# Two fused linear layers on one core: another order of ScalarE's and VectorE's work in batches 1 and 2

## The chip, the cores and the metric

The kernel runs on one core of one Trainium2 chip. A core has a matrix engine (TensorE, PE in the profile), three elementwise engines (VectorE or DVE, ScalarE or ACT, GpSimd or POOL) and a queue (SyncE, SP) that here only issues DMAs. Each engine takes its own list of instructions in the order in which the program wrote it, and waits on counters (semaphores) that the others raise. The metric is the device time of one launch in microseconds (us). Before the change it is 382.21 us, the median of 3 runs (381.04 to 382.56).

## The reference

For each of 8 batches, x is 256 x 1024 in float32. Two residual layers follow each other:

```python
sign = 2 * mask - 1                       # int32 mask, 1024 x 1024 for each batch
x = x + (x @ W0.T + b0 + (x @ sign) * coeff[batch])
A, B = lora_As[id[batch]], lora_Bs[id[batch]]      # 1024 x 16 and 16 x 1024
x = x + (x @ W1.T + b1 + (x @ A) @ B * 2.0)
```

## The kernel before

**Arithmetic.** A float32 operand is split into a high part (rounded to the type float32r, which the matrix engine takes) and a low part (the rest), and a product is the sum high*high + high*low + low*high. ScalarE makes nearly all high parts, VectorE the low parts; every low part waits for its high part. The residual is folded in as the identity added to the weights ("diagonal" blocks, added by GpSimd at line 389, or by VectorE in `w22_diagonal`).

**Layer 0** of a batch needs its own weights, because the mask is the batch's own: W0 + 2*coeff*mask - coeff. They come in 8 units of 128 x 1024, through a ring of 6 slots. For each unit, VectorE makes the sum (`weights_sum`, line 999), ScalarE the high part (`weights_high`, line 702), VectorE the low part (`weights_low`, line 1009), and the matrix engine uses it (lines 519 and 525). Units 0 to 3 give the first half of the output y, units 4 to 7 the second. A slot's next transfer is issued when the matrix engine has read the slot. The ready y leaves the matrix engine's banks by `y_copy` (ScalarE, L740) and `y_sum` (VectorE, L1081), and is split by `y_high...` (ScalarE, L748 in batch 1, L758 later) and `y_low...` (VectorE, L1087 in batch 1, L1116 later). The second halves of the batch's banks wait for the copies of the batch before (`z_copy`, L780).

**Layer 1** multiplies y by W1. In batches 0 and 1 it does that plainly, from batch 2 on by Strassen's scheme in Winograd's form, with 7 block products in place of 8 (L550); they use T1 to T4, which are sums and differences of quarters of W1. These are made once, in batches 1 and 2, each in two halves c = 0, 1: `t_sum` (VectorE, L1057), `t_high` (ScalarE, L724), `t_low` (VectorE, L1062). In the Winograd layer of batch 2, the products take T3 second, T4 fourth, T1 fifth and T2 sixth. `t_lo_done` counts the low parts, so the list `T_ORDER` has to name the order in which they are made.

**The low-rank part.** The matrix engine makes h = y @ A (L561), between the products. ScalarE scales and splits h by three small instructions (`h_high`, L765), VectorE makes its low part (`h_low`, L1122), and then one product for each output block adds h @ B and closes the block (`close`, L591). GpSimd prepares A and B's low parts (`lora_a_diff` L401, `lora_a_low` L406, `lora_b_low` L415), between two ScalarE instructions, `lora_a_high` (L792) and `lora_b_copy` (L800). `z_copy` (batches 0 and 1) moves a closed block out of its bank.

The order on each engine is written out by hand for batches 0 to 2, and by `next_high` and `next_low` with the loops behind them for the rest. The change touches only the hand-written lists for batches 1 and 2; the lists of PE, GpSimd and SP stay as they are.

Of the kernel before, what the change touches and what calls it, by code (L numbers as in the profile page):

```python
# [17 lines left out]
def cond_residual_two_layers(nc, x, cols, slot_ids, mask, w0, w1, b1, lora_a, lora_b, out):  # L18
# [11 lines left out]
    KT = XG * PAIR  # L30
# [17 lines left out]
    W11, W12, W21, W22, T1, T2, T4 = range(7)  # L48
    T3 = W12
    T_SUMS = [(T1, k) for k in range(HT)] + [(T3, 0), (T2, 0), (T3, 1), (T2, 1), (T4, 0), (T4, 1)]  # L50
    T_ORDER = [(T1, 0), (T1, 1)] + [(t, c) for c in range(2) for t in (T2, T3, T4)]

    with ExitStack() as ctx:
        def sb(name, shape, dt):
# [642 lines left out]
        def _(act):  # L697
            def weights_high(b, k):
                e = entry(b, k)
                for lo, hi in ((0, HALF), (HALF, D)) if b == 0 and k < HALVED else ((0, D),):  # L700
                    act.wait_ge(sum_done, parts(b, k, lo // HALF))
                    act.activation(wc_hi[:, e % RING, lo:hi], sums[:, e % RING, lo:hi], ACT.Identity,  # L702
                                   bias=coeff_neg[:, b:b + 1]).then_inc(wc_hi_done, 1)
# [12 lines left out]
            def t_high(t, c):  # L716
                act.wait_ge(t_sum_done, t_sums(t, PAIR * c + 1 if t == T1 else c))
                if t == T3:
                    act.wait_ge(w12_read, 1)
                elif t == T4:  # L720

                    act.wait_ge(t_lo_done, t_count(T3, c))
                ks = slice(PAIR * c, PAIR * (c + 1))
                act.activation(w1_two[0][:, t, ks, :], t_raw(t)[:, ks, :], ACT.Copy).then_inc(t_hi_done, 1)  # L724

            def x_high(b, g):
                g = pair(b, g)
                act.wait_ge(x_in[g], 16 * (b + 1))
                act.activation(x_two[:, g, 0], x_raw[:, g], ACT.Copy).then_inc(x_hi_done, 1)  # L729
# [30 lines left out]
            def h_high(b):  # L760

                act.wait_ge(h_full, b + 1)
                hs = h_bank(b)[:].rearrange("p (s n t) -> p n s t", s=ST, n=2)
                for lo, hi, n in ((0, 2 * R, 0), (2 * R, 4 * R, 1), (B_HI, B_ALL, 0)):
                    act.activation(by_rows(h_stack[lo:hi, :]), hs[0:hi - lo, n], ACT.Copy,  # L765
                                   scale=SCALING).then_inc(h_hi_done, 1)
# [9 lines left out]
            def z_copy(b, i):  # L776
                act.wait_ge(z_full, 4 * b + z_place(b, i))
                s, _ = z_rows_of(b, i)
                need(act, z_out[s], 16 * b)
                act.activation(z_piece(b, i), layer1_bank(b, i)[:], ACT.Copy).then_inc(z_done, 1)  # L780
# [70 lines left out]
            x_high(1, 0)  # L851
            x_high(1, 1)
            weights_high(1, 1)
            x_high(1, 2)
            x_high(1, 3)
            h_high(0)
            weights_high(1, 2)
            weights_high(1, 3)
            for i in range(4):
# [22 lines left out]
            y_high_pair(1, 2)  # L882
            y_high_pair(1, 3)
            lora_b_copy(1, 1)
            t_high(T2, 0)
            for u in range(3):
                weights_high(2, u)
            h_high(1)
            weights_high(2, 3)
            for g in range(XG):  # L890
                x_high(2, g)
            t_high(T3, 0)
            z_copy(1, 0)
            weights_high(2, 4)
            z_copy(1, 1)
            t_high(T4, 0)
            weights_high(2, 5)
            z_copy(1, 2)
            t_high(T2, 1)
            t_high(T3, 1)  # L900
            z_copy(1, 3)


            weights_high(2, KT - 2)
# [6 lines left out]
            y_copy(2, 3)  # L911
            y_high(2, Y11)
            y_high(2, S3)
            t_high(T4, 1)
            lora_a_high(2)


# [66 lines left out]
        def _(dve):  # L984
# [207 lines left out]
            w1_low(HT + 3)  # L1192
            x_low(1, 0)
            weights_low(1, 0)
            x_low(1, 1)
            h_low(0)
            weights_low(1, 1)
            weights_sum(1, 2)
            x_low(1, 2)
# [18 lines left out]
            t_sum(T3, 0)  # L1218
            t_sum(T2, 0)
            t_low(T1, 0)  # L1220


            for o in range(HT, KT):
                y_sum(1, o)
            w22_diagonal(1)
            t_sum(T3, 1)
            y_low_pair(1, 2)
            y_low_pair(1, 3)
            weights_sum(2, 0)
            t_sum(T2, 1)  # L1230
            weights_sum(2, 1)
            weights_low(2, 0)
            weights_sum(2, 2)
            weights_low(2, 1)
            weights_low(2, 2)
            h_low(1)
            weights_sum(2, 3)
            t_sum(T4, 0)
            for g in range(XG):
                x_low(2, g)  # L1240
            weights_low(2, 3)
            t_low(T1, 1)
            t_sum(T4, 1)
            t_low(T2, 0)
            weights_sum(2, 4)
            t_low(T3, 0)
            weights_low(2, 4)
            weights_sum(2, 5)
            t_low(T4, 0)
            weights_low(2, 5)  # L1250


            weights_sum(2, KT - 2)
            t_low(T2, 1)
            weights_low(2, KT - 2)
            weights_sum(2, KT - 1)
            for o in range(HT):
                y_sum(2, o)
            y_add(2, S3)
            weights_low(2, KT - 1)  # L1260
            t_low(T3, 1)
            y_low(2, Y11)
            y_low(2, S3)


            for o in range(HT, KT):
                y_sum(2, o)
            y_add(2, S1)
            t_low(T4, 1)
            y_low(2, V12)  # L1270
            y_add(2, S2)
            y_low(2, Y22)
            y_low(2, S1)
# [84 lines left out]
```

## Time and profile before

| | before |
| --- | --- |
| median of 3 runs | 382.21 us |
| the profiled execution, its own time | 381.96 us |
| its span, first to last instruction | 379.0 us |
| granted TensorE clock | 1.000 of full speed |
| PE busy | 370.2 us (98%) |
| DVE busy | 310.0 us (82%) |
| ACT busy | 204.6 us (54%) |
| POOL busy | 93.2 us (25%) |
| DMA | mean 250 GB/s |

Times in the timeline are us from the span's start. A row of the timeline has the start, the time from the first start to the last end, the engine, the source line, the operation with its tiles and shapes, and the count. A bracket at its end gives the idle time of the engine before it, and what ended that. A matrix product's own duration holds about 0.16 us of pipeline that the next product overlaps, so what a wait costs is read from start to start. Batch 1's first layer starts at 59.5 us, its second at 81.9; batch 2's first layer at 107.7, its second at 131.2.

### The profile page before, as it was taken

The page shows a single profiled execution, that of the slowest core. Times are in us where ns is not written, and L with a number is a line of the kernel's source. Part 1 is how long each engine was busy: PE and PEld are TensorE (multiplying, and loading weights), DVE is VectorE, ACT ScalarE, POOL GpSimd, SP SyncE. Part 2 cuts the span into 40 slices and gives each one's busy share as a digit, 9 for nine tenths or more (in the row PEclk, how much of TensorE's full clock was granted, in tenths as well). Part 3 has the DMA queues.
Part 4 walks back from the last instruction along what each step waited for, and adds up shares of the span by engine and source line. Part 5 has one row for each costly group of instructions (what it writes and reads, how often), then busy time and mean ns, then how long its engine had stood idle before and what let it go on. Part 6 is the DMA issues. An engine that isn't in the chain of part 4 may idle for free.

```text
span 379.0 us, 5435 instructions
## 1 busy us (share of the span) xinstructions
PE 370.2 (98%) x1934; PEld 311.7 (82%) x1934; DVE 310.0 (82%) x372; ACT 204.6 (54%) x315; POOL 93.2 (25%) x116
## 2 busy tenths in 40 slices
PE   7999999999999999999999999999999999999996
PEld 7889977887787887888788887888878887888875
DVE  4998899988999899976897769965999659987613
ACT  5583865656547577347652666524673366526520
POOL 1355660434004521033100350012300431002300
PEclk9999999999999999999999999999999999999999
DMA  8999999999539587495937959297884969473002
GB/s 249 389 386 341 384 386 331 309 370 315 211 106 305 203 293 261 138 346 198 339 145 247 350 177 359 81 285 270 266 297 124 329 216 335 164 253 129 0 0 111
DMA packets 47691, 94.73 MB, mean 250 GB/s; under 512 B 3610, under 2 KB 4658, under 8 KB 47666
## 3 DMA queue, kind: packets, MB, share of 16 engines
q1 hardware_dynamic: 44848, 85.73, 67.1%
q10 hardware_dynamic: 2754, 8.66, 5.7%
q8 instruction: 15, 0.25, 0.3%
q14 instruction: 10, 0.08, 0.1%
q0 software_dynamic: 64, 0.01, 0.0%
HBM read 86.00 MB, written 8.39 MB: 249 GB/s over the span
## 4 chain that ended last, share of the span: by engine, by line
PE 79%; DVE 7%; DMA 5%; issue 4%; ACT 2%; SPq 1%; POOL 1%; DVEq 0%; ACTq 0%; POOLq 0%
PE bank L550 30%; PE bank L519 22%; PE bank L525 11%; PE bank L599 6%; PE bank L561 3%; DMA ring_raw<-in_w 3%; DVE ring_raw L999 3%; PE bank L467 2%; PE bank L591 2%; DMA ring_raw<-in_mask 1%; PE bank L474 1%; ACT ring L702 1%; DVE ring L1009 1%; POOL ring_raw L389 1%; DVE x_two L1068 1%
## 5 line engine op out<-in xcount | busy, mean ns | idle before, releaser
L550 PE MATMUL bank<-w_two,y_two 128*128 128x512 f32 x600 | 141.5, 390 | 0.1
L702 ACT ACTIVATE ring<-ring_raw,coeff_neg 128x1024 fp32r<-128x1024 f32 (+1 forms) x68 | 75.0, 1103 | 115.1 <-DVE ring_raw L999 114.6
L550 PEld LDWEIGHTS bank<-w_two,y_two 128*128 128x128 f32 x600 | 111.6, 188 | 23.9 <-issue 0.3
L519 PE MATMUL bank<-x_two,ring 128*128 128x512 f32 x448 | 127.1, 394 | 0.8 <-ACT z_rows L780 0.8
L389 POOL TENSOR_TENSOR ring_raw<-ring_raw,ident 128x128 f32<-128x128 f32 x64 | 46.8, 752 | 222.2 <-DMA ring_raw<-in_w 221.9
L999 DVE SCALAR_TENSOR_TENSOR ring_raw<-ring_raw,coeff_two 128x1024 f32<-128x1024 int32 (+1 forms) x68 | 84.9, 1261 | 15.0 <-DMA ring_raw<-in_mask 12.8
L1009 DVE SCALAR_TENSOR_TENSOR ring<-ring_raw,coeff_neg,ring 128x1024 fp32r<-128x1024 f32 (+1 forms) x68 | 84.1, 1245 | 9.7 <-ACT ring L702 9.0
L519 PEld LDWEIGHTS bank<-x_two,ring 128*128 128x128 f32 x448 | 78.0, 189 | 12.8 <-ACT z_rows L780 1.2
L525 PE MATMUL bank<-x_two,ring 128*128 128x256 f32 x448 | 78.0, 281 | 0.0
L525 PEld LDWEIGHTS bank<-x_two,ring 128*128 128x128 f32 x448 | 70.6, 189 | 8.3
L1081 DVE TENSOR_TENSOR y_raw<-bank,y_raw 128x256 f32<-128x256 f32 x56 | 20.7, 418 | 21.1 <-ACT y_raw L740 21.1
L1116 DVE TENSOR_TENSOR y_two<-y_raw,y_two 128x512 fp32r<-128x512 f32 x42 | 31.3, 767 | 5.3 <-ACT y_two L758 5.2
L415 POOL TENSOR_TENSOR b_stack<-b_raw,b_tmp 16x512 fp32r<-16x512 f32 x16 | 25.5, 1593 | 21.1 <-ACT b_tmp L800 20.5
L758 ACT ACTIVATE y_two<-y_raw 128x512 fp32r<-128x512 f32 x42 | 24.8, 625 | 4.6 <-DVE y_raw L1081 3.4
L740 ACT ACTIVATE y_raw<-bank,cols_all 128x256 f32<-128x256 f32 x56 | 21.9, 470 | 2.9 <-PE bank L525 2.8
L599 PE MATMUL bank<-w_two,y_two 128*128 128x512 f32 x96 | 22.6, 391 | 0.0
L1068 DVE TENSOR_TENSOR x_two<-x_both,x_two 128x512 fp32r<-128x512 f32 x32 | 21.7, 702 | 0.6 <-ACT x_two L729 0.6
L599 PEld LDWEIGHTS bank<-w_two,y_two 128*128 128x128 f32 x96 | 17.8, 188 | 4.0 <-DVE w_two L1025 0.4
L467 PE MATMUL bank<-x_two,ring 128*128 128x256 f32 x128 | 18.5, 285 | 1.2 <-ACT ring L702 0.7
L729 ACT ACTIVATE x_two<-x_both 128x512 fp32r<-128x512 f32 x32 | 18.3, 615 | 2.1 <-DMA x_both<-in_x 2.1
L774 ACT ACTIVATE z_rows<-bank 128x512 f32<-128x512 f32 x18 | 10.7, 597 | 15.5 <-PE bank L550 15.3
L1143 DVE TENSOR_TENSOR z_rows<-bank,z_rows 128x512 f32<-128x512 f32 x24 | 15.9, 684 | 3.7 <-PE bank L591 3.7
(50 smaller groups left out, 241.6 us busy)
## 6 DMA issues: line engine op xcount, KB each, us to landing
ring_raw<-in_w SPq DMA_DIRECT2D x60, 512.0 KB, 8.6
ring_raw<-in_mask SPq DMA_DIRECT2D x60, 512.0 KB, 9.7
x_both<-in_x SPq DMA_DIRECT2D x31, 256.0 KB, 4.0
out<-z_rows ACTq DMA_DIRECT2D x15, 512.0 KB, 7.5
w_raw<-in_w SPq DMA_DIRECT2D x12, 512.0 KB, 11.4
b_raw<-in_lora_b SPq DMA_DIRECT2D x8, 448.0 KB, 3.6
ring_raw<-in_w SPq DMA_DIRECT2D x8, 256.0 KB, 6.1
ring_raw<-in_mask SPq DMA_DIRECT2D x8, 256.0 KB, 6.2
```

The costliest lines, as they stand in the source:

```text
L389: ins = pool.tensor_tensor(blk, blk, ident[:], ALU.add)
L415: pool.tensor_tensor(b_stack[B_HI:B_ALL, cols], b_raw[B_HI:B_ALL, cols], b_tmp[B_HI:B_ALL, :].bitcast(F32), ALU.subtract).then_inc(b_lo_do ...
L467: pe.matmul(first_bank(o), w, x_two[:, pair(0, u), n, i, :], start=(u % HT == 0 and i == 0 and n == 0), stop=False, skip_group_check=True)
L519: pe.matmul(layer0_bank(b, o)[:, 0:2 * T], w, x_two[:, k // PAIR, :, k % PAIR, :], start=(k == 0), stop=False, skip_group_check=True)
L525: ins = pe.matmul(layer0_bank(b, o)[:, 0:T], w, x_two[:, k // PAIR, 0, k % PAIR, :], start=False, stop=(k == KT - 1), skip_group_check=True)
L550: ins = pe.matmul(bank[:], y_two[:, q, k, yp, :], w1_two[wp][:, j, k, :], start=(start and k == 0 and n == 0), stop=False, skip_group_chec ...
L599: pe.matmul(layer1_bank(0, i)[:], y_two[:, PAIR * h + s, k % HT, yp, :], w1_two[wp][:, PAIR * h + half, k % HT, :], start=(k == 0 and yp = ...
L702: act.activation(wc_hi[:, e % RING, lo:hi], sums[:, e % RING, lo:hi], ACT.Identity, bias=coeff_neg[:, b:b + 1]).then_inc(wc_hi_done, 1)
L999: dve.scalar_tensor_tensor(out=sums[:, e % RING, lo:hi], in0=mask_at[:, e % RING, lo:hi], scalar=coeff_two[:, b:b + 1], in1=w0_at[:, e % R ...
L1009: dve.scalar_tensor_tensor(out=wc_lo[:, e % RING, lo:hi], in0=sums[:, e % RING, lo:hi], scalar=coeff_neg[:, b:b + 1], in1=wc_hi[:, e % RIN ...
L1068: dve.tensor_tensor(x_two[:, g, 1], x_raw[:, g], x_two[:, g, 0].bitcast(F32), ALU.subtract).then_inc(x_lo_done, 1)
L1116: dve.tensor_tensor(y_two[:, n, :, 1, :], y_raw[:, at, :, 1, :], y_two[:, n, :, 0, :].bitcast(F32), ALU.subtract).then_inc(y_lo_done, 1)
```

## The change

All moves are within ScalarE's and VectorE's lists. Batch 1: `h_high(0)` stands right behind `weights_high(1, 1)`, ahead of two parts of x, and `h_low(0)` ahead of `x_low(1, 1)`. Batch 2's preparation: `h_high(1)` comes after two of the weights' high parts instead of three, `h_low(1)` after two low parts instead of three; the four `z_copy(1, ...)` stand behind each other before `weights_high(2, 4)`; `w22_diagonal(1)` and `t_sum(T3, 1)` stand before the `y_sum`s of batch 1's second half instead of after them; `weights_sum(2, 0)` stands before `y_low_pair(1, 2)`. T2's high and low parts, which stood second, are made last, in batch 2; T3's second half comes early.

```diff
@@ -48,7 +48,7 @@
     W11, W12, W21, W22, T1, T2, T4 = range(7)
     T3 = W12
     T_SUMS = [(T1, k) for k in range(HT)] + [(T3, 0), (T2, 0), (T3, 1), (T2, 1), (T4, 0), (T4, 1)]
-    T_ORDER = [(T1, 0), (T1, 1)] + [(t, c) for c in range(2) for t in (T2, T3, T4)]
+    T_ORDER = [(t, c) for t in (T1, T3, T4, T2) for c in range(2)]
 
     with ExitStack() as ctx:
         def sb(name, shape, dt):
@@ -851,9 +851,9 @@
             x_high(1, 0)
             x_high(1, 1)
             weights_high(1, 1)
+            h_high(0)
             x_high(1, 2)
             x_high(1, 3)
-            h_high(0)
             weights_high(1, 2)
             weights_high(1, 3)
             for i in range(4):
@@ -882,23 +882,22 @@
             y_high_pair(1, 2)
             y_high_pair(1, 3)
             lora_b_copy(1, 1)
-            t_high(T2, 0)
-            for u in range(3):
-                weights_high(2, u)
+            weights_high(2, 0)
+            weights_high(2, 1)
             h_high(1)
+            weights_high(2, 2)
             weights_high(2, 3)
             for g in range(XG):
                 x_high(2, g)
             t_high(T3, 0)
             z_copy(1, 0)
+            t_high(T3, 1)
+            for i in range(1, 4):
+                z_copy(1, i)
             weights_high(2, 4)
-            z_copy(1, 1)
             t_high(T4, 0)
             weights_high(2, 5)
-            z_copy(1, 2)
-            t_high(T2, 1)
-            t_high(T3, 1)
-            z_copy(1, 3)
+            t_high(T4, 1)
 
 
             weights_high(2, KT - 2)
@@ -911,7 +910,8 @@
             y_copy(2, 3)
             y_high(2, Y11)
             y_high(2, S3)
-            t_high(T4, 1)
+            t_high(T2, 0)
+            t_high(T2, 1)
             lora_a_high(2)
 
 
@@ -1192,8 +1192,8 @@
             w1_low(HT + 3)
             x_low(1, 0)
             weights_low(1, 0)
+            h_low(0)
             x_low(1, 1)
-            h_low(0)
             weights_low(1, 1)
             weights_sum(1, 2)
             x_low(1, 2)
@@ -1218,56 +1218,56 @@
             t_sum(T3, 0)
             t_sum(T2, 0)
             t_low(T1, 0)
+            w22_diagonal(1)
+            t_sum(T3, 1)
 
 
             for o in range(HT, KT):
                 y_sum(1, o)
-            w22_diagonal(1)
-            t_sum(T3, 1)
+            weights_sum(2, 0)
             y_low_pair(1, 2)
             y_low_pair(1, 3)
-            weights_sum(2, 0)
-            t_sum(T2, 1)
             weights_sum(2, 1)
             weights_low(2, 0)
             weights_sum(2, 2)
             weights_low(2, 1)
+            h_low(1)
+            t_sum(T2, 1)
+            weights_sum(2, 3)
             weights_low(2, 2)
-            h_low(1)
-            weights_sum(2, 3)
-            t_sum(T4, 0)
+            t_low(T1, 1)
             for g in range(XG):
                 x_low(2, g)
             weights_low(2, 3)
-            t_low(T1, 1)
+            t_sum(T4, 0)
+            weights_sum(2, 4)
             t_sum(T4, 1)
-            t_low(T2, 0)
-            weights_sum(2, 4)
+            weights_low(2, 4)
             t_low(T3, 0)
-            weights_low(2, 4)
             weights_sum(2, 5)
+            t_low(T3, 1)
+            weights_low(2, 5)
             t_low(T4, 0)
-            weights_low(2, 5)
 
 
             weights_sum(2, KT - 2)
-            t_low(T2, 1)
+            t_low(T4, 1)
             weights_low(2, KT - 2)
             weights_sum(2, KT - 1)
             for o in range(HT):
                 y_sum(2, o)
+            weights_low(2, KT - 1)
             y_add(2, S3)
-            weights_low(2, KT - 1)
-            t_low(T3, 1)
             y_low(2, Y11)
             y_low(2, S3)
+            t_low(T2, 0)
 
 
             for o in range(HT, KT):
                 y_sum(2, o)
             y_add(2, S1)
-            t_low(T4, 1)
             y_low(2, V12)
+            t_low(T2, 1)
             y_add(2, S2)
             y_low(2, Y22)
             y_low(2, S1)
```

**ScalarE (ACT), end of batch 1's y and batch 2's first weights.** Before; L702 is a high part of weights, L765 are h's parts, L780 copies of z, L724 high parts of T.

```order
L800 ACTIVATE b_tmp<-b_raw_59 16x512
L724 ACTIVATE w1_two0_51<-w1_raw1_50 128x1024
L702 ACTIVATE ring_54<-ring_raw_53,coeff_neg 128x1024 x3
L765 ACTIVATE h_stack<-bank5 32x256 x2
L765 ACTIVATE h_stack<-bank5 16x256
L702 ACTIVATE ring_54<-ring_raw_53,coeff_neg 128x1024
L729 ACTIVATE x_two_56<-x_both_55 128x512 x4
L724 ACTIVATE w1_two0_51<-w1_raw0_49 128x1024
L780 ACTIVATE z_rows_61<-bank1 128x512
L702 ACTIVATE ring_54<-ring_raw_53,coeff_neg 128x1024
L780 ACTIVATE z_rows_61<-bank2 128x512
```

The same place after, to the last copy of z.

```order
L800 ACTIVATE b_tmp<-b_raw_59 16x512
L702 ACTIVATE ring_54<-ring_raw_53,coeff_neg 128x1024 x2
L765 ACTIVATE h_stack<-bank5 32x256 x2
L765 ACTIVATE h_stack<-bank5 16x256
L702 ACTIVATE ring_54<-ring_raw_53,coeff_neg 128x1024 x2
L729 ACTIVATE x_two_56<-x_both_55 128x512 x4
L724 ACTIVATE w1_two0_51<-w1_raw0_49 128x1024
L780 ACTIVATE z_rows_61<-bank1 128x512
L724 ACTIVATE w1_two0_51<-w1_raw0_49 128x1024
L780 ACTIVATE z_rows_61<-bank2 128x512
L780 ACTIVATE z_rows_61<-bank3 128x512
L780 ACTIVATE z_rows_61<-bank4 128x512
```

T2's high part and one of weights' have gone from in front of h's parts, and the last copy of z no longer stands behind two high parts of weights.

**VectorE (DVE), end of batch 1's second half of y**, the difference. L1081 is a `y_sum`, L1033 and L1057 are the diagonal and `t_sum(T3, 1)`, L999 is `weights_sum(2, 0)`, L1087 the low parts of y.

```order
-L1081 TENSOR_TENSOR y_raw_57<-bank5,y_raw_57 128x2x128
-L1081 TENSOR_TENSOR y_raw_57<-bank6,y_raw_57 128x2x128
-L1081 TENSOR_TENSOR y_raw_57<-bank7,y_raw_57 128x2x128
-L1081 TENSOR_TENSOR y_raw_57<-bank0,y_raw_57 128x2x128
 L1033 TENSOR_TENSOR w1_raw1_50<-w1_raw1_50,ident 128x128 x2
 L1057 TENSOR_TENSOR w1_raw0_49<-w1_raw1_50,w1_raw0_49 128x1024
+L1081 TENSOR_TENSOR y_raw_57<-bank5,y_raw_57 128x2x128
+L1081 TENSOR_TENSOR y_raw_57<-bank6,y_raw_57 128x2x128
+L1081 TENSOR_TENSOR y_raw_57<-bank7,y_raw_57 128x2x128
+L1081 TENSOR_TENSOR y_raw_57<-bank0,y_raw_57 128x2x128
+L999 SCALAR_TENSOR_TENSOR ring_raw_53<-ring_raw_53,coeff_two 128x1024
 L1087 TENSOR_TENSOR y_two_58<-y_raw_57,y_two_58 128x2x2x128 x2
```

The diagonal and the sum have moved ahead of the y sums, and one sum of weights ahead of y's low parts.

**ScalarE, batch 2, between the two halves of y**, after the change. L740 are copies of y, L758 high parts of y, L724 high parts of T2, L792 is `lora_a_high`.

```order
L740 ACTIVATE y_raw_57<-bank0,cols_all 128x2x128
L758 ACTIVATE y_two_58<-y_raw_57 128x4x128 x2
L724 ACTIVATE w1_two0_51<-w1_raw1_50 128x1024 x2
L792 ACTIVATE a_parts<-a_raw 128x12x16
L740 ACTIVATE y_raw_57<-bank1,cols_all 128x2x128
```

Before, one L724 stood there, T4's second half; now two do, both of T2. On VectorE, `weights_low(2, 7)` has moved ahead of `y_add(2, S3)`, on which the second L758 waits.

## Rows read from the trace of the kernel before

**Rows 1.** The page: busy us, share of the span and instructions of each engine.
```profile
PE 370.2 (98%) x1934; PEld 311.7 (82%) x1934; DVE 310.0 (82%) x372; ACT 204.6 (54%) x315; POOL 93.2 (25%) x116
```

**Rows 2.** Timeline of PE (start, length, engine, line, operation, count, idle before).
```profile
55.09 2.90 PE L599 MATMUL bank<-w_two,y_two 128*128 128x512 f32 x12
58.47 1.18 PE L591 MATMUL bank<-b_stack,h_stack 128*128 128x512 f32 x4 [0.48 <-issue]
...
81.89 11.10 PE L550 MATMUL bank<-w_two,y_two 128*128 128x512 f32 x48
92.83 2.02 PE L561 MATMUL bank<-y_two,a_parts 128*32 128x512 f32 x8
94.69 5.63 PE L550 MATMUL bank<-w_two,y_two 128*128 128x512 f32 x24
101.22 0.47 PE L591 MATMUL bank<-b_stack,h_stack 128*128 128x512 f32 x1 [0.90 <-ACT h_stack L765]
...
118.89 0.86 PE L519 MATMUL bank<-x_two,ring 128*128 128x512 f32 x3
120.56 0.50 PE L519 MATMUL bank<-x_two,ring 128*128 128x512 f32 x1 [0.82 <-ACT z_rows L780]
...
143.95 5.63 PE L550 MATMUL bank<-w_two,y_two 128*128 128x512 f32 x24
149.79 0.47 PE L591 MATMUL bank<-b_stack,h_stack 128*128 128x512 f32 x1 [0.21 <-issue]
```

**Rows 3.** Timeline of VectorE, batch 1.
```profile
57.95 0.42 DVE L1122 SCALAR_TENSOR_TENSOR h_stack<-bank,h_stack 32x256 fp32r<-32x256 f32 x1
...
86.68 1.52 DVE L1081 TENSOR_TENSOR y_raw<-bank,y_raw 128x256 f32<-128x256 f32 x4 [2.40 <-ACT y_raw L740]
88.12 0.56 DVE L1033 TENSOR_TENSOR w_raw<-w_raw,ident 128x128 f32<-128x128 f32 x2
...
89.86 1.79 DVE L1087 TENSOR_TENSOR y_two<-y_raw,y_two 128x512 fp32r<-128x512 f32 x1
91.56 0.68 DVE L1087 TENSOR_TENSOR y_two<-y_raw,y_two 128x512 fp32r<-128x512 f32 x1
92.17 1.27 DVE L999 SCALAR_TENSOR_TENSOR ring_raw<-ring_raw,coeff_two 128x1024 f32<-128x1024 int32 x1
```

**Rows 4.** Timeline of GpSimd at that place.
```profile
81.89 3.71 POOL L389 TENSOR_TENSOR ring_raw<-ring_raw,ident 128x128 f32<-128x128 f32 x4 [8.79 <-DMA ring_raw<-in_w]
...
84.73 0.88 POOL L389 TENSOR_TENSOR ring_raw<-ring_raw,ident 128x128 f32<-128x128 f32 x2
...
89.60 1.50 POOL L415 TENSOR_TENSOR b_stack<-b_raw,b_tmp 16x512 fp32r<-16x512 f32 x1 [1.27 <-ACT b_tmp L800]
```

**Rows 5.** Timeline of VectorE, batch 2.
```profile
104.17 2.50 DVE L1068 TENSOR_TENSOR x_two<-x_both,x_two 128x512 fp32r<-128x512 f32 x4 [0.60 <-ACT x_two L729]
...
122.98 1.48 DVE L999 SCALAR_TENSOR_TENSOR ring_raw<-ring_raw,coeff_two 128x1024 f32<-128x1024 int32 x1
...
126.04 0.79 DVE L1081 TENSOR_TENSOR y_raw<-bank,y_raw 128x256 f32<-128x256 f32 x2 [0.92 <-ACT y_raw L740]
126.86 0.69 DVE L1111 TENSOR_TENSOR y_raw<-y_raw 128x512 f32<-128x512 f32 x1
...
149.27 0.41 DVE L1122 SCALAR_TENSOR_TENSOR h_stack<-bank,h_stack 32x256 fp32r<-32x256 f32 x1
```

**Rows 6.** Timeline of ScalarE, batches 1 and 2.
```profile
55.47 1.13 ACT L729 ACTIVATE x_two<-x_both 128x512 fp32r<-128x512 f32 x2
56.51 1.15 ACT L765 ACTIVATE h_stack<-bank 32x256 fp32r<-32x256 f32 x3
...
99.25 1.15 ACT L765 ACTIVATE h_stack<-bank 32x256 fp32r<-32x256 f32 x3
...
130.31 1.06 ACT L724 ACTIVATE w_two<-w_raw 128x1024 fp32r<-128x1024 f32 x1 [2.10 <-DVE w_two L1062]
...
131.53 1.55 ACT L740 ACTIVATE y_raw<-bank,cols_all 128x256 f32<-128x256 f32 x4
```

## The prediction

> **What bounds the kernel now.** I read the page first. PE is busy 98% of the span [rows 1], at the full clock, and the change leaves PE's own list as it is. So only the waits of PE in batches 1 and 2 can be won. The list of PE's waits names them (h's parts, a copy of z, and "issue"), and PE's timeline, which I take next, places them and shows what they cost from start to start; its brackets alone, 0.48, 0.90, 0.82 and 0.21 us, leave out 0.16 us each [rows 2]. The 48 products from 81.89 to 92.83 us are 0.228 us apart. By that step:
> - the close of batch 0 could start at 55.09 + 12 x 0.228 = 57.82 us and starts at 58.47: 0.65 us. It starts right behind `h_low`, at 57.95 + 0.42 = 58.37 us [rows 3].
> - the close of batch 1: 94.69 + 24 x 0.228 = 100.16, starts at 101.22: 1.06 us. This is h's parts on ScalarE, which started only at 99.25 us [rows 6], although the low-rank products ended about 94.7.
> - the fourth bank in batch 2's second half: 118.89 + 3 x 0.233 = 119.59, starts at 120.56: 0.97 us, the last copy of z. (0.233 is these products' step: the row's three end at 119.75, 0.86 us from the start, 0.40 of it one product's own.)
> - the close of batch 2: 143.95 + 24 x 0.228 = 149.42, starts at 149.79: 0.37 us, behind the `h_low` of 149.27 [rows 5].
>
> Together 3.05 us, of which 2.68 lie in the first three. That is the ceiling of any reordering in this stretch. The reader is to see a second thing: VectorE is nearly as full. From 92.17 to 122.98 us it has one idle piece of mark, 0.60 us [rows 3, 5]. Whatever PE wins, VectorE has to follow.
>
> **Batch 0's h.** `h_high(0)` waits no more behind two parts of x. In the row its three instructions start at 56.51 us, 1.04 us behind the start of the two x parts (two of 0.52), so they can start about 55.5 [rows 6]. VectorE's `h_low(0)` then passes `x_low(1, 1)`, one of about 0.7 us: 57.95 becomes 57.24, its end 57.66, before the 57.82 at which PE is ready. Gain 0.65 us. x's parts move back by about 1.15 us; PE asks for them a unit of weights or two later, and I cost that at nothing: even if the cover were gone, it costs those 1.15 us at most.
>
> **Batch 1's y, the filled idle time.** VectorE idles 2.40 us before the four `y_sum`s at 86.68 us, because ScalarE's copies wait behind `lora_a_high`, that for GpSimd's `lora_a_diff`, and that stands behind two diagonals of batch 2's unit 1. The diagonal (from 88.12) and `t_sum(T3, 1)` (to 89.86) [rows 3] are 1.74 us, and would fit in the hole, from 84.28 to 86.02. But GpSimd works in this hole. Of the four diagonals in the row, the last two, with VectorE idle, took 0.88 us; the first two, beside VectorE's sums, filled the 2.84 us from 81.89 to 84.73 [rows 4]. So `lora_a_diff` is late by between 0 and 2.84 - 0.88 = 1.96 us. I take 0.6: VectorE's two short instructions come first, some 0.3 us each, and two of GpSimd's go between. The idle piece goes, but its end moves from 86.68 to 87.3.
>
> Here a rule of the Trainium skill bears (SBUF — State Buffer, "Who interferes with whom"): a VectorE instruction with two SBUF inputs and a GpSimd one that reads SBUF exclude each other for the whole instruction, and who issues first decides. The trace agrees: `y_low_pair(1, 2)` took 1.79 us beside GpSimd's 1.50, and its like 0.68 without [rows 3, 4]. By the rule an unlucky order of issue gives rival 3 below; were the port only shared in proportion, the diagonals would be late by a part, and the 0.4 us below would be 0.
>
> Then: four y sums, 1.44 us, to 88.75; `weights_sum(2, 0)`, 1.2 us (1.27 at 92.17, overlapping the next a little), and some 0.15 of collision, to 90.1; the two low parts of y as in the rows, 1.70 and 0.61, to 92.4, say 92.5 us. Before they ended at 92.2. PE wants them for the low-rank products, now at 92.83 - 0.65 = 92.18 us. So a new wait of about 0.4 us arises here (0 if GpSimd isn't delayed, 1.7 if it is by the whole 1.96).
>
> **Batch 1's h.** From 92.5: `weights_sum(2, 1)`, low, sum, low are 4 x 1.2 = 4.8 us, and `h_low(1)` comes at 97.3 us instead of 100.70. ScalarE has h's parts done by about 96, behind the low-rank products. PE closes at 100.16 - 0.65 + 0.4 = 99.9: nothing waits, gain 1.06 us. The weights (2, 2) and (2, 3) come later relative to h, but PE starts batch 2 only at about 106; covered by 5 us.
>
> **The copies of z.** All four stand behind T3's high parts and are done by about 107.5, the last block closing at about 106.5; PE asks for the fourth bank at 118. Gain 0.97 us. `weights_high(2, 4)` comes behind them and loses nothing, as it stands behind its sum, at 107 to 108.5.
>
> **VectorE to batch 2's last unit.** The stretch 92.17 to 122.98 is 30.81 us. Out of it go `weights_sum(2, 0)` (1.2) and the idle 0.60, as ScalarE's x parts are earlier. T2's two low parts leave, T3's and T4's second come in: the same cost. So `weights_sum(2, 7)` starts at 92.5 + 29.0 = 121.5 us, 1.5 earlier; its transfer is gated by PE and is in time.
>
> **T2 last, and the two halves of y.** From that sum on: the second pair of `y_sum`s follows 3.06 us later (122.98 to 126.04), so at 124.6, and ends at 125.4. Now `weights_low(2, 7)`, 1.2, comes before `y_add(S3)`, 0.69: 127.3 [rows 5]. ScalarE: a high part of y, 0.6, then a half of T2, some 1.0, then the other half and `lora_a_high`, together 1.22 as from 130.31 to 131.53, then the copies of y's second half. That gives 130.1 us, and 130.5 if GpSimd's diagonals, of which two fall there, cost VectorE 0.2 us each; before it was 131.53 [rows 6]. This chain moves by 1.0 to 1.4 us, and I take 1.0, while PE by then is 0.65 - 0.4 + 1.06 + 0.97 = 2.3 us ahead.
>
> From there VectorE's list has the same length as before, with T2's low part in T4's place: 17.7 us from 131.53 to `h_low(2)` at 149.27. PE's close moves with it: 149.79 - 1.0 = 148.8 us. What PE had over, 1.3 us, comes back as waits for y's parts (near 138 us) and for h (near 148). Behind 150 us PE had no wait of mark, and all engines are 1.0 us earlier together.
>
> **Sum.** -0.65 + 0.4 - 1.06 - 0.97 + 1.3 = -1.0 us on the profiled execution's 381.96 us (span 379.0 and 3.0 around it), 381.0 us. That execution lies 0.25 us below the median of the runs; I set 381.1 us.
>
> **Rivals.**
> 1. Everything is kept. VectorE and ScalarE follow, and all four waits go: 381.96 - 3.05 = 378.9 us. For it: GpSimd's delay can be nil. Against: the chain over T2's high parts hangs on `y_add`, not on GpSimd. 12%.
> 2. VectorE is the bound. The collisions with GpSimd between 113 and 127 us fall worse, or the T2 pair and `weights_low(2, 7)` ahead of `y_add` cost what the filled hole gave, and the copies of y come at 131.5 again: 382.0 us. For it: the hand sum leaves that chain only 1.0 us. 19%.
> 3. Slower: the collision at 84 to 92 us at full price. `lora_a_diff` late by 1.96, y's sums at 88.6, to 90.1; the sum of weights to 91.3; both low parts of y caught by `lora_b_low`, 1.70 each, to 94.7 us, 2.2 behind my 92.5. PE waits 2.5 us, and the chain behind is 2.2 - 1.0 = 1.2 later than before: 383.2 us. It decides from the point where y's last low part ends after 92.5 + 1.0 = 93.5 us. For it: the 1.79 us row. Against: GpSimd has one such instruction there, not two. 9%. By the skill's rule that the lock is held for the whole instruction, this is the price, too; only the order of issue saves it.
>
> **Numbers.** Forecast 60%, its own range 380.3 to 381.8. A measurement of this kernel can tell 0.5% (1.9 us) from no change: faster means under 380.3, slower over 384.1. Faster: rival 1 and a tail of the forecast, 0.19. Slower: half of rival 3's spread, 0.05. Same: 0.76. The range reaches part of the way to rival 1 and to rival 3: 379.6 to 382.7.
>
> **What would show it.** Right: no PE idle time before the closes near 58 and 100 us, and before the fourth bank near 118; GpSimd's diagonals near 84.7 longer than 0.88 for two; a short wait of PE before the products with `a_parts` near 92.6; the copies of y in batch 2 at 130.5 and PE's wait before the close near 148.8 above 1 us. Wrong: that last wait not grown (rival 1), the copies of y at 131.5 (rival 2), or y's last low part of batch 1 behind 93.5 us (rival 3).

## The result, and the profile after

The changed kernel takes 379.06 us (median of 9 runs, 377.99 to 379.48), the kernel before, beside it, 381.04 us (9 runs, 380.15 to 382.73): ratio 0.9948, interval 0.9929 to 0.9967, so 2.0 us faster. I had forecast 381.1 us and 1.0 us faster; the time lies below the range. The three runs known at the forecast (median 382.21), and the profiled execution of before (381.96), were among the slower ones: beside the later experiments, in four sets of 28 to 30 runs, its median was 380.8 to 381.1 us.

The profiled execution of the changed kernel took 378.78 us, its span is 376.1, 2.9 us less than before. This pair of profiles overstates the change. Over all runs the median span is 377.0 us for the changed kernel (375.9 to 377.4) and, in the four later sets, 378.5 to 378.7 for the one before, so the span shortened by 1.5 to 1.8 us. The profile's page, in its first part, against [rows 1]:

```profile
PE 369.3 (98%) x1934; PEld 311.6 (83%) x1934; DVE 311.2 (83%) x372; ACT 205.1 (55%) x315; POOL 95.9 (25%) x116
```

The same work; GpSimd is busy 2.7 us longer, which is time in which it is held up. PE's timeline (start, length, engine, line, operation, count, idle before), against [rows 2]:

```profile
54.98 2.91 PE L599 MATMUL bank<-w_two,y_two 128*128 128x512 f32 x12
57.77 1.16 PE L591 MATMUL bank<-b_stack,h_stack 128*128 128x512 f32 x4
...
81.21 11.11 PE L550 MATMUL bank<-w_two,y_two 128*128 128x512 f32 x48
92.16 2.02 PE L561 MATMUL bank<-y_two,a_parts 128*32 128x512 f32 x8
94.01 5.63 PE L550 MATMUL bank<-w_two,y_two 128*128 128x512 f32 x24
99.48 0.40 PE L591 MATMUL bank<-b_stack,h_stack 128*128 128x512 f32 x1
...
117.09 1.09 PE L519 MATMUL bank<-x_two,ring 128*128 128x512 f32 x4
...
128.30 11.08 PE L550 MATMUL bank<-w_two,y_two 128*128 128x512 f32 x48
...
141.07 5.63 PE L550 MATMUL bank<-w_two,y_two 128*128 128x512 f32 x24
146.91 0.71 PE L591 MATMUL bank<-b_stack,h_stack 128*128 128x512 f32 x2 [0.21 <-issue]
```

The reader is to see three brackets gone: before 57.77, before 99.48, and inside the four products of 117.09. No new one stands at 92.16, where I had expected 0.4 us. Batch 2's second layer starts at 128.30 instead of 131.18 us, 2.88 earlier, and at 146.91 the old wait of 0.37 us from start to start (141.07 + 24 x 0.228 = 146.54) is as long as before, not 1.3 us longer. In the second profile of this kernel (after_again, below) it is 0.86 us.

VectorE, against [rows 3] and [rows 5]:

```profile
57.25 0.42 DVE L1122 SCALAR_TENSOR_TENSOR h_stack<-bank,h_stack 32x256 fp32r<-32x256 f32 x1
...
84.43 0.87 DVE L1033 TENSOR_TENSOR w_raw<-w_raw,ident 128x128 f32<-128x128 f32 x2
85.33 1.23 DVE L1057 TENSOR_TENSOR w_raw<-w_raw,w_raw 128x1024 f32<-128x1024 f32 x1
86.48 1.41 DVE L1081 TENSOR_TENSOR y_raw<-bank,y_raw 128x256 f32<-128x256 f32 x4
87.81 1.66 DVE L999 SCALAR_TENSOR_TENSOR ring_raw<-ring_raw,coeff_two 128x1024 f32<-128x1024 int32 x1
89.39 2.38 DVE L1087 TENSOR_TENSOR y_two<-y_raw,y_two 128x512 fp32r<-128x512 f32 x2
91.69 1.27 DVE L999 SCALAR_TENSOR_TENSOR ring_raw<-ring_raw,coeff_two 128x1024 f32<-128x1024 int32 x1
...
120.43 1.27 DVE L999 SCALAR_TENSOR_TENSOR ring_raw<-ring_raw,coeff_two 128x1024 f32<-128x1024 int32 x1
...
123.28 0.79 DVE L1081 TENSOR_TENSOR y_raw<-bank,y_raw 128x256 f32<-128x256 f32 x2 [0.92 <-ACT y_raw L740]
...
125.18 0.68 DVE L1111 TENSOR_TENSOR y_raw<-y_raw 128x512 f32<-128x512 f32 x1
...
146.39 0.42 DVE L1122 SCALAR_TENSOR_TENSOR h_stack<-bank,h_stack 32x256 fp32r<-32x256 f32 x1
```

The hole of 2.40 us is full. The y sums start at 86.48 (I had 87.3), y's low parts end at 91.8 (92.5), `weights_sum(2, 7)` starts at 120.43 (121.5). GpSimd, against [rows 4]:

```profile
82.44 2.39 POOL L389 TENSOR_TENSOR ring_raw<-ring_raw,ident 128x128 f32<-128x128 f32 x2 [1.68 <-DMA ring_raw<-in_w]
84.78 0.37 POOL L401 TENSOR_TENSOR a_raw<-a_raw 128x64 f32<-128x64 f32 x1
```

The two diagonals of batch 2's unit 1 took 2.39 us where they had taken 0.88; that they would take longer was forecast. But they started at 82.44 instead of 84.73: the DMA ended the wait, and in this execution it landed 2.3 us earlier. 1.0 us of this is that the transfer was issued at 70.17 instead of 71.21 us, 1.3 that it took 12.2 instead of 13.5 us. ScalarE, against [rows 6]:

```profile
126.43 1.99 ACT L724 ACTIVATE w_two<-w_raw 128x1024 fp32r<-128x1024 f32 x2
128.33 0.35 ACT L792 ACTIVATE a_parts<-a_raw 128x192 fp32r<-128x192 f32 x1
128.58 1.55 ACT L740 ACTIVATE y_raw<-bank,cols_all 128x256 f32<-128x256 f32 x4
```

The copies of y come at 128.58; I had 130.5.

### The profile page after: what moved, and what is told of

Read it like the earlier page. It is cut to its first block, busy times and chain, and to the rows that moved or that the text cites. A ratio compares the mean times of both kernels' runs of the same rounds, so it can differ in the third digit from the quotient of the medians.

```text
span 376.1 us, 5435 instructions
## 1 busy us (share of the span) xinstructions
PE 369.3 (98%) x1934; PEld 311.6 (83%) x1934; DVE 311.2 (83%) x372; ACT 205.1 (55%) x315; POOL 95.9 (25%) x116
## 4 chain that ended last, share of the span: by engine, by line
PE 94%; DMA 2%; SPq 2%; DVE 1%; issue 1%; POOL 0%; ACT 0%; DVEq 0%
PE bank L550 36%; PE bank L519 28%; PE bank L525 14%; PE bank L599 6%; PE bank L561 4%; PE bank L467 2%; PE bank L591 2%; DMA ring_raw<-in_w 2%; PE bank L474 1%; SPq L306 1%; SPq L307 1%; DVE ring_raw L999 1%; DVE ring L1009 0%; SPq L325 0%; POOL ring_raw L389 0%
## 5 line engine op out<-in xcount | busy, mean ns | idle before, releaser
L702 ACT ACTIVATE ring<-ring_raw,coeff_neg 128x1024 fp32r<-128x1024 f32 (+1 forms) x68 | 75.0, 1103 | 110.5 <-DVE ring_raw L999 109.9
L389 POOL TENSOR_TENSOR ring_raw<-ring_raw,ident 128x128 f32<-128x128 f32 x64 | 50.0, 801 | 217.3 <-DMA ring_raw<-in_w 217.3
L999 DVE SCALAR_TENSOR_TENSOR ring_raw<-ring_raw,coeff_two 128x1024 f32<-128x1024 int32 (+1 forms) x68 | 84.6, 1258 | 13.5 <-DMA ring_raw<-in_mask 11.0
L1009 DVE SCALAR_TENSOR_TENSOR ring<-ring_raw,coeff_neg,ring 128x1024 fp32r<-128x1024 f32 (+1 forms) x68 | 84.2, 1246 | 9.7 <-ACT ring L702 8.9
L519 PEld LDWEIGHTS bank<-x_two,ring 128*128 128x128 f32 x448 | 78.0, 189 | 11.6
L525 PEld LDWEIGHTS bank<-x_two,ring 128*128 128x128 f32 x448 | 70.7, 189 | 8.4
L1081 DVE TENSOR_TENSOR y_raw<-bank,y_raw 128x256 f32<-128x256 f32 x56 | 20.6, 417 | 19.3 <-ACT y_raw L740 19.3
L1116 DVE TENSOR_TENSOR y_two<-y_raw,y_two 128x512 fp32r<-128x512 f32 x42 | 32.1, 786 | 5.3 <-ACT y_two L758 5.0
L758 ACT ACTIVATE y_two<-y_raw 128x512 fp32r<-128x512 f32 x42 | 24.9, 624 | 6.5 <-DVE y_raw L1081 3.4
L740 ACT ACTIVATE y_raw<-bank,cols_all 128x256 f32<-128x256 f32 x56 | 22.0, 470 | 3.0 <-PE bank L525 3.0
L467 PEld LDWEIGHTS bank<-x_two,ring 128*128 128x128 f32 x128 | 16.7, 191 | 2.0 <-DVE x_two L1068 1.9
```

The costliest lines, as they stand in the source:

```text
L389: ins = pool.tensor_tensor(blk, blk, ident[:], ALU.add)
L467: pe.matmul(first_bank(o), w, x_two[:, pair(0, u), n, i, :], start=(u % HT == 0 and i == 0 and n == 0), stop=False, skip_group_check=True)
L519: pe.matmul(layer0_bank(b, o)[:, 0:2 * T], w, x_two[:, k // PAIR, :, k % PAIR, :], start=(k == 0), stop=False, skip_group_check=True)
L525: ins = pe.matmul(layer0_bank(b, o)[:, 0:T], w, x_two[:, k // PAIR, 0, k % PAIR, :], start=False, stop=(k == KT - 1), skip_group_check=True)
L758: act.activation(y_two[:, n, :, 0, :], y_raw[:, at, :, 1, :], ACT.Copy).then_inc(y_hi_done, 1)
L999: dve.scalar_tensor_tensor(out=sums[:, e % RING, lo:hi], in0=mask_at[:, e % RING, lo:hi], scalar=coeff_two[:, b:b + 1], in1=w0_at[:, e % R ...
```

## The experiments

Two theories stood after the result. "Cap" (also "landing"): my chain was right, and the change gained more only since the units landed early in its executions. "Kept": the chain has room at any landing. All ratios are to the kernel before, run beside on the same chip. A ratio need not be the quotient of the two medians; where the difference matters, the text says so. The changed kernel again gave:

> The changed kernel once more, as the mark for the others. Theory 'cap' (ScalarE's and VectorE's chain to the copies of y in batch 2 limits what PE keeps; in the profiled execution it was fast only because the weights of batch 2's unit 1 landed 2.3 us earlier than in the profile of before): the landing varies between executions, ratio to before 0.995 to 0.998. Theory 'kept' (the chain has room, all of 2.7 to 3.1 us are kept): 0.992 to 0.995.

378.91 us, ratio 0.9949 (0.9929 to 0.9969), span 376.5. Diagonals at 82.2, copies of y at 128.9 us. The ratio lies where the two ranges meet and decides nothing.

**Parts of the change undone.**

> The changed kernel, but VectorE's diagonal, t_sum(T3, 1) and weights_sum(2, 0) are back behind the y sums and the y low parts of batch 1. 'Cap': VectorE is late by the 1.2 to 1.7 us that the idle time had taken in, the copies of y in batch 2 come at about 130 instead of 128.6, and the kernel is 1.2 to 1.7 us slower than the changed one, nearly all of its gain lost. 'Kept': VectorE has room, at most 0.4 us slower.

```diff
-            w22_diagonal(1)
-            t_sum(T3, 1)
             for o in range(HT, KT):
                 y_sum(1, o)
-            weights_sum(2, 0)
+            w22_diagonal(1)
+            t_sum(T3, 1)
             y_low_pair(1, 2)
             y_low_pair(1, 3)
+            weights_sum(2, 0)
```

380.95 us, ratio 1.0002 (0.9984 to 1.0021), apart from the changed kernel's interval: 2.0 us lost in the medians, 1.8 in the median spans (378.7 against 376.9). "Cap" had said 1.2 to 1.7, "kept" at most 0.4. The diagonals are as early (82.6) as in the changed kernel, and PE starts batch 2's second layer as early (128.21 us), but the copies of y come at 129.94, and the waits that I had forecast for the changed kernel stand here, before a product of y and before the close of batch 2 (148.25, 1.22 us from start to start). PE of this kernel:

```profile
136.88 3.00 PE L550 MATMUL bank<-w_two,y_two 128*128 128x512 f32 x12 [0.30 <-issue]
139.72 2.01 PE L561 MATMUL bank<-y_two,a_parts 128*32 128x512 f32 x12
148.25 0.70 PE L591 MATMUL bank<-b_stack,h_stack 128*128 128x512 f32 x2 [1.06 <-issue]
```

So VectorE's list is a bound, and the filled hole is what lets it follow.

> The changed kernel, but h_high(1) again behind three high parts of weights and h_low(1) behind three low parts, as before. If the place of h is what removed the wait of 1.06 us at batch 1's close, it comes back in part: h_low would end at about 98.5 us, PE asks at 99.5, so I expect no wait and no difference (within 0.3 us) under both theories; a rival, that h's place alone did it, says 1 us slower.

```diff
             weights_high(2, 1)
-            h_high(1)
             weights_high(2, 2)
+            h_high(1)
...
             weights_low(2, 1)
-            h_low(1)
-            t_sum(T2, 1)
-            weights_sum(2, 3)
             weights_low(2, 2)
+            h_low(1)
+            t_sum(T2, 1)
+            weights_sum(2, 3)
```

380.11 us, ratio 0.9975 (0.9955 to 0.9995), 1.2 us slower by the medians, where I had expected no difference; the intervals overlap. Its profile has no wait at batch 1's close, as expected. But on VectorE the idle 0.60 us of [rows 5] is back, which neither the changed kernel nor z_off has, and from the first y sum of batch 1's second half to the third of batch 2 it takes 37.6 us, where the changed kernel takes 36.8. So batch 1's h brings something by its place, through VectorE's list and not through the wait that I had counted for it. The diagonals started at 86.41 us, with no collision (0.87), and PE waited for y's low parts, the wait that I had forecast. VectorE, and PE:

```profile
104.13 2.50 DVE L1068 TENSOR_TENSOR x_two<-x_both,x_two 128x512 fp32r<-128x512 f32 x4 [0.60 <-ACT x_two L729]
```

```profile
93.45 2.05 PE L561 MATMUL bank<-y_two,a_parts 128*32 128x512 f32 x8 [0.63 <-DVE y_two L1087]
```

> The changed kernel, but the copies of z of batch 1 stand between the high parts of weights and of T again. The last one would be done at about 115.5 us, PE asks at 116.7: no difference (within 0.3 us) if VectorE's earlier sums are what released it; 0.5 to 1.0 us slower if the copies' place is what removed the wait of 0.97 us.

```diff
             z_copy(1, 0)
-            t_high(T3, 1)
-            for i in range(1, 4):
-                z_copy(1, i)
             weights_high(2, 4)
+            z_copy(1, 1)
+            t_high(T3, 1)
             t_high(T4, 0)
             weights_high(2, 5)
+            z_copy(1, 2)
             t_high(T4, 1)
+            z_copy(1, 3)
```

379.78 us, ratio 0.9968 (0.9952 to 0.9983): 0.9 us above the changed kernel by the medians, but the intervals overlap, so this tells neither "no difference" nor the 0.5 to 1.0 us of the other reading. No wait on a copy of z in its profile; its diagonals started at 86.04, late again.

**The landing moved on purpose.** A second profile of the kernel before:

> The kernel before once more, for a second profile. 'Landing' (the profile of before was one in which the transfers of batch 1's units 2 and 3 and of batch 2's first two units were slow): here batch 2's unit 1 may land near 82 instead of 84.4 us; then the copies of y in batch 2 come about 130.5 to 131.5 and the span is 377.8 to 378.6. Theory 'kept' says that landing moves nothing: span 379.0 within 0.3.

One run, 382.0 us, span 380.0, and the diagonals at 86.0: the landing was later still, and neither expected span came. PE then waited 0.74 us for y's low parts and 1.44 for h. "Early" moves the two quarters of W1 for T4 (1 MB) behind batch 2's units 0 and 1 on the DMA queue; "late" puts 1 MB of transfers that nothing uses in front. The first part of the diff is "early" (the two lines leave their old place, lower down), the second "late". The added lines shift the line numbers by 1 in the early kernels and by 4 to 5 in the late ones: L565 there is the L561 of before.

```diff
                 for u in range(PAIR):
                     load_weights(b, u)
+                if b == FIRST:
+                    for c in range(2):
+                        load_quarter(T4, c, 0, w21_in[c])
...
                         load_quarter(T4, c, 0, w21_in[c])
+                    for n in range(2):
+                        sp.dma_start(spare[n], w0[n]).then_inc(spare_in, 16)
```

> The kernel before, but batch 2's units 0 and 1 are loaded ahead of the two quarters of W1 for T4, 1 MB, so they land 2.7 us earlier. 'Landing': lora_a_diff and with it the y sums and VectorE's list move forward: 0.3 to 1.0 us faster than before, and the upper tail of the runs (382 to 383) gets thinner. Rival (VectorE works back to back behind it, the landing is covered): no difference.

> The changed kernel with the same earlier loads. 'Landing': GpSimd's diagonals are done long before VectorE fills the hole, no collision; 0.2 to 0.6 us faster than the changed one (ratio to before 0.993 to 0.995), as in the fast landing little is left to win. Rival: no difference.

> The changed kernel with 1 MB of additional transfers (W0's first two blocks, copied within HBM) in front of batch 2's first units, so that these land 2.7 us later than in its profile, as late as in the profile of before or later. 'Landing' (my forecast's wait at the low-rank products and the delay of VectorE's list were right, only the landing was earlier): the wait of PE on y's low parts near 92.6 us comes, 0.5 to 2 us, and the kernel is 1.0 to 2.0 us slower than the changed one, ratio to before 0.998 to 1.001. 'Kept': within 0.4 us of the changed one.

before_early: 379.80 us, 0.9971 (0.9952 to 0.9990), so 1.2 us from the order of the transfers alone (0.3 to 1.0 expected). after_early: 378.58, 0.9949 (0.9933 to 0.9965), as the changed kernel. late2: 381.92, 1.0030 (1.0004 to 1.0055), 3 us slower than the changed kernel (1.0 to 2.0 expected), with PE's forecast wait before the low-rank products (1.73 us at 94.16). The landing matters; is it the reason for my error? The four once more, side by side:

> The kernel before with the same 1 MB of additional transfers in front of batch 2's first units as in late2. If VectorE's list is what sets the pace, it is late here as well: 3 us slower than before (ratio 1.007 to 1.010), and the change gains 1.0 to 2.0 us against it. If the change made the kernel alone sensitive to the landing (its hole now filled), this one is at most 1 us slower than before, and late2 is as slow or slower.

> late2 once more, the changed kernel with late units: ratio to before 1.000 to 1.005. Against before_late2: 1.0 us faster if the forecast's sum holds for a late landing, 2.0 or more if it undervalues the change at any landing.

> before_early once more, the kernel before with batch 2's first units 1 MB earlier: ratio to before 0.996 to 0.998.

> after_early once more: ratio to before 0.994 to 0.995, so 0.8 to 1.2 us faster than before_early_b: at an early landing the change brings less, since GpSimd's diagonals are out of the way in both.

| units of batch 2 | before | changed | gain |
| --- | --- | --- | --- |
| 1 MB late | 384.45 us, 1.0072 (1.0046 to 1.0098) | 381.76 us, 1.0008 (0.9975 to 1.0040) | 2.7 us |
| as they are | 381.04 us | 379.06 us, 0.9948 (0.9929 to 0.9967) | 2.0 us |
| 1 MB early | 380.15 us, 0.9971 (0.9949 to 0.9994) | 378.64 us, 0.9926 (0.9898 to 0.9954) | 1.5 us |

The gains are differences of the medians; the middle row is the first measurement. The change gains at every landing, also at a late one, where I had put its danger. That it gains more there isn't shown for certain: by the ratios the three gains are 2.4, 2.0 and 1.7 us, with intervals that overlap. The median spans point the same way: 3.4 us (382.2 and 378.8), 1.5 to 1.8, and 1.1 (377.6 and 376.5). Single profiles are no measure of it: those of before_early_b and after_early_b have spans of 377.0 and 376.7 us, those of before_early and after_early 378.0 and 377.0. before_late2 shows where a late landing hurts. Its rows of VectorE and PE:

```profile
90.64 1.52 DVE L1086 TENSOR_TENSOR y_raw<-bank,y_raw 128x256 f32<-128x256 f32 x4 [6.52 <-ACT y_raw L744]
```

```profile
96.24 2.04 PE L565 MATMUL bank<-y_two,a_parts 128*32 128x512 f32 x8 [3.12 <-DVE y_two L1092]
...
105.16 0.47 PE L595 MATMUL bank<-b_stack,h_stack 128*128 128x512 f32 x1 [1.40 <-ACT h_stack L769]
...
124.42 0.50 PE L523 MATMUL bank<-x_two,ring 128*128 128x512 f32 x1 [0.73 <-ACT z_rows L784]
```

and of late2_b, GpSimd, VectorE and PE:

```profile
87.39 0.88 POOL L393 TENSOR_TENSOR ring_raw<-ring_raw,ident 128x128 f32<-128x128 f32 x2 [2.59 <-DMA ring_raw<-in_w]
```

```profile
89.34 1.52 DVE L1086 TENSOR_TENSOR y_raw<-bank,y_raw 128x256 f32<-128x256 f32 x4 [2.93 <-ACT y_raw L744]
```

```profile
94.41 2.04 PE L565 MATMUL bank<-y_two,a_parts 128*32 128x512 f32 x8 [1.68 <-DVE y_two L1092]
...
150.14 0.71 PE L595 MATMUL bank<-b_stack,h_stack 128*128 128x512 f32 x2 [1.10 <-issue]
```

The unit landed 1.3 us later in before_late2 than in late2_b, so not all of the difference between the two is the change's. The diagonals are undisturbed (0.88 us): at 87.4 us VectorE has finished what fills the hole and idles until the sums, 2.93 us. So a landing that is late enough excludes a collision. Near the landing that I had assumed, 84.7 us, it doesn't. h2_only (below), which has the changed kernel's lists up to the h of batch 2, landed at 84.0, the two diagonals ran to 85.9 and took 1.9 us instead of 0.88, and the y sums started at 87.23:

```profile
81.31 4.59 POOL L389 TENSOR_TENSOR ring_raw<-ring_raw,ident 128x128 f32<-128x128 f32 x4 [8.71 <-DMA ring_raw<-in_w]
```

```profile
87.23 1.41 DVE L1081 TENSOR_TENSOR y_raw<-bank,y_raw 128x256 f32<-128x256 f32 x4
```

In fill_only (below) the unit landed at 84.2, the two took 0.93 us, and the sums started at 86.46.

**Single moves on the kernel before, and one more.**

> The kernel before with the move of batch 0's h alone. PE's wait of 0.65 us before batch 0's close goes. 'Kept': 0.65 us faster, ratio 0.998. 'Cap': what follows (landing, GpSimd, VectorE's list) isn't moved by it, PE waits more later: no difference.

381.37 us, ratio 1.0006 (0.9985 to 1.0026): no gain, as "cap" had said. The wait before batch 0's close is gone, and the one before batch 1's has grown from 0.90 to 1.44 us, h's low part being made at the old time (100.6):

```profile
101.11 0.47 PE L591 MATMUL bank<-b_stack,h_stack 128*128 128x512 f32 x1 [1.44 <-ACT h_stack L765]
```

> The kernel before with only the diagonal and t_sum(T3, 1) ahead of batch 1's y sums and weights_sum(2, 0) ahead of its y low parts. Taking these moves out of the changed kernel cost it all of its 2.0 us. If VectorE's list sets the pace by itself: 1.0 to 1.5 us faster than before, as h is made earlier by as much. If it works only together with the other moves (h behind three weights and one part of T2 still): 0 to 0.5 us.

380.79 us, ratio 0.9985 (0.9963 to 1.0007), not told from before, though its profiled execution has a span of 377.3 and no wait at batch 1's close. How much this part brings alone stays open. Together with fill_off it says that the filled hole is needed for the gain, not that it suffices.

> The changed kernel, and from batch 2 on h_high stands ahead of the next batch's first two parts of x on ScalarE, and h_low ahead of x_low, weights_sum, x_low on VectorE. Theory 'chain' (what is left is PE's wait for h at batch 2's close, 0.2 to 0.7 us, since VectorE's list reaches h_low late): 0.3 to 0.7 us faster than the changed kernel, ratio to before about 0.9935. Rival: the wait moves to the next product (p_added, or the copies), no difference.

> The same, and batch 2's first two units loaded ahead of T4's quarters. 'Landing' and 'chain' together: 0.5 to 1.0 us faster than the changed one, ratio to before 0.992 to 0.994, the best of all versions. Rival: as the changed one, 0.995.

380.15 us, 0.9949 (0.9927 to 0.9972; the medians' quotient is 0.9978), and 379.38 us, 0.9947 (0.9923 to 0.9970): no better than the changed kernel. `h_low(2)` starts at 145.43 us, earlier than in the changed kernel, and the wait for h is gone, but the next product waits for `p_add`, 1.26 us in h2_only, as the rival said:

```profile
149.12 1.63 PE L550 MATMUL bank<-w_two,y_two 128*128 128x512 f32 x6 [1.26 <-DVE z_rows L1131]
```

No version was shown to beat the changed kernel; the lowest ratio, 0.9926, is after_early_b's, but after_early, the same kernel, gave 0.9949. No run undoes the order of T2's parts alone.

## Why the prediction was wrong

The step that failed is the term of the sum "1.3 us comes back as waits". I let VectorE's and ScalarE's chain to the copies of y, and with it PE's close of batch 2, move by only 1.0 us, while PE was 2.3 us ahead. In the two profiles of the changed kernel the copies came at 128.58 and 128.94 us and not at 130.5, and of what PE had won 0.0 and 0.5 us came back before the close of batch 2 (a wait of 0.37 and 0.86 us from start to start, 0.37 before). Over all runs the span shortened by 1.5 to 1.8 us, so for the typical execution the gain lies between my 1.0 us and the 2.9 of the profiles.

The mechanism was right: PE's waits, and behind them one chain over VectorE, ScalarE and GpSimd that takes back what it can't follow. fill_off shows it, where the waits come back with 0.30 and 1.22 us and the gain is gone. What was wrong is the size of this chain. The profiles show how the lists hang together by a constant: the last matrix product starts 226.2 us after `h_low(2)` in every kernel but h2_only and h2_early. So the gain of the profile is what `h_low(2)` moves: 149.27 to 146.39 us, 2.88. `h_low(2)` is a mark of where the lists stand, and not by itself the cause: in h2_only it was moved ahead by another 1.0 us, the last product came 228.6 us behind it, and nothing was gained. Starts in us, each from one profile:

| kernel | diagonals of unit (2, 1) | first y_sum, batch 1's second half | third y_sum of batch 2 | copies of y, second half | h_low(2) |
| --- | --- | --- | --- | --- | --- |
| forecast for after | 84.7 | 87.3 | 124.6 | 130.5 | 148.3 |
| before | 84.7 | 86.7 | 126.0 | 131.5 | 149.3 |
| before_again | 86.0 | 88.0 | 127.3 | 132.4 | 150.2 |
| before_late2 | 88.7 | 90.6 | 129.9 | 135.1 | 152.8 |
| before_early_b | 80.1 | 84.7 | 124.2 | 129.5 | 147.2 |
| after | 82.4 | 86.5 | 123.3 | 128.6 | 146.4 |
| after_again | 82.2 | 86.4 | 123.4 | 128.9 | 146.7 |
| late2_b | 87.4 | 89.3 | 125.9 | 131.8 | 149.6 |
| after_early_b | 80.7 | 85.9 | 122.7 | 129.1 | 146.9 |

Point by point:
- **Batch 0's h: right in its place, wrong as a term.** The wait went, but alone (h0_only) it brings nothing. What it is worth beside the other moves no run tells.
- **"I take 0.6", the delay of `lora_a_diff`: its size stays open, and the y sums came 0.8 us earlier than I had them.** In after the sums start at 86.48 right behind VectorE's own `t_sum(T3, 1)`: the collision was real (2.39 us for the pair), but the unit had landed 2.3 us earlier. In the late executions nothing collides, and the sums follow 1.95 us after the diagonals' start, as before (late2_b and h1_off 1.95). For a landing as I assumed it, 84.7, the nearest rows are 86.46 (fill_only) and 87.23 (h2_only), so my 87.3 could have come. The fault was to take the landing of one execution for that of all.
- **VectorE to batch 2's third y sum: sized 37.3 us, measured 36.8** in after, 36.5 to 37.0 in the six profiles of the changed kernel as it is, early and late; before 39.4. Taking `weights_sum(2, 0)` and the 0.60 us out was right. The 0.5 us too much lie behind y's low parts: 0.3 up to `weights_sum(2, 7)`, and 0.2 behind it, as that sum took 1.27 us in after and 1.48 in before.
- **T2 last, the copies of y: sized 5.9 us, measured 5.3** in after, 5.5 in before. The pair of T2's high parts starts right behind y's high part (126.43) and replaces a wait of 2.10 us for `t_low(T3, 1)` [rows 6]. Of the 0.6 us, 0.4 is the reserve that I took for GpSimd and that this execution didn't need. Others did: 6.0 in late2_b, 6.4 in after_early_b, where ScalarE waits 0.5 and 0.9 us for GpSimd. The six profiles give 5.7 on average, so as a size for all executions this term was right.
- **"1.3 us comes back as waits": failed as what these three lead to.** They are 0.8 + 0.5 + 0.6 = 1.9 us too late for the profile of after, so that its chain moved 2.9 us and not 1.0. The first and the last hang on the execution; only the middle one shows in all six, with 0.3 to 0.8 us.
- **The copies of z and batch 1's h: right** that both waits go. That their own new places did it isn't shown: with either back in the old place the wait didn't return in the profile. The place of batch 1's h counts in another way, by the 0.60 us of VectorE that came back in h1_off.
- **The base.** My sum amounts to a span of 378.0 us and 3.0 us outside it. The changed kernel's medians are 377.0 and 2.1 us, and those of the kernel before are 378.5 to 378.7 and 2.1 to 2.6. So about half of the miss in time is that I took one execution's 3.0 us outside the span for the rule, and half is the span.

Rival 1 (everything kept, 12%) has the time, 378.9 us, that was measured within 0.2, but by luck: it takes 3.05 us off a base that is 1 us too high, and 2.0 us were gained. Its mechanism, that VectorE and ScalarE simply follow, holds nearly for the profile of after and not in general, as fill_off shows. Rival 3 had its wait (0.63 to 1.73 us at the low-rank products in late executions) but not its place: the kernel before waits there longer, 3.12 us.

What chooses the landing stays open. It isn't the change alone: before had 84.7 and 86.0, h0_only 84.6, fill_only 84.2; the changed kernel 82.4 and 82.2, but h1_off and z_off 86.4 and 86.0. Of the time outside the span (2.0 to 3.9 us over all runs) I can say nothing either.

## What to carry to other kernels

Here one engine is busy 98% of the span and a second 97% of a stretch (VectorE 30.0 of the 30.8 us from 92.2 to 123): that makes two critical paths. Find a mark at which both lists stand at a constant distance from the end (here `h_low(2)`), and count each move by how it shifts that mark; a wait removed upstream brought nothing by itself here. Moving the mark's own instruction ahead doesn't help, as h2_only shows. Before joining two costs in one sum, ask for which landings both can hold. A time that begins with a DMA's landing needs a second profile, or two bounds, before it carries a term. And the spans of many runs tell the gain better than one pair of profiles.

## What the runs showed of the hardware

The same transfer, the second unit of batch 2, landed between 82.1 us (after_again) and 86.4 us (h1_off) in ten profiles of kernels with the same DMA order, and 84.7 and 86.0 in the two of the kernel before. Counted from its issue it took 12.0 us (after_again) to 15.3 us (h1_off).

VectorE and GpSimd hold each other up there: two GpSimd additions of 128x128 took 0.88 us with VectorE idle, 2.39 us beside it, while VectorE's two of that shape took 0.87 instead of 0.56. The Trainium skill says that a VectorE instruction with two SBUF inputs contends with a GpSimd one that reads SBUF (SBUF — State Buffer, "Who interferes with whom"), and the trace agrees. In after this cost VectorE's list 0.3 us at this place. The larger price stood elsewhere, and not in every execution: between the halves of batch 2's y ScalarE waited 0.5 us for GpSimd in after_early, late2_b, fill_off and h2_only, and 0.9 us in after_early_b.
